# Attention steps that exponentiate heads in pairs and score four at a time, in place of groups of three

## The chip, the cores and the metric

One core of a Trainium2 chip runs the whole program. The metric is the device time of one execution in microseconds (us). Times "into the span" count from the first profiled instruction.

## The reference

An attention layer and a mixture-of-experts layer read the same normalised rows, and both are added to the input. Cut to what matters:

```python
xn = layernorm(x)                               # x: (4, 1024, 128)
q, k, v = heads(xn @ Wq.T), heads(xn @ Wk.T), heads(xn @ Wv.T)   # 16 heads of 8
q, k = rope(q), rope(k)
attn = softmax(einsum('bhnd,bhmd->bhnm', q, k) * 8 ** -0.5)
x = x + einsum('bhnm,bhmd->bhnd', attn, v) + moe(xn)   # 8 experts, 3 layers, top 2 by a gate
```

For each batch (4) and head (16), 1024 x 1024 scores are exponentiated: 67 million exponentials, all on ScalarE save some that VectorE takes in the last steps.

## The kernel before

**Steps and blocks.** Attention runs in 16 steps: a step is one batch and four of its heads. A step has 16 blocks (`BLOCKS`), numbered j: two halves of 512 queries, and in each half eight tiles of 128 keys. A block is one tile of keys against 512 queries for four heads. Its scores are four matmuls that contract 32 rows each (one head in each quarter of TensorE's rows) into 512 columns of a PSUM bank apiece; they are exponentiated by ScalarE from PSUM into `probs`; and its values are matmuls (eight in the trace, two for each head) that add the weighted values, and the sums by which to divide, into one bank (`o_ps`) that runs through the step.

**Steps 0 and 1** handle a block as two pairs of heads. `scores` (L1494 to L1519) writes the four heads of a block into two slots of two banks: pair 0 always into the same slot, pair 1 into one of two others in turn. It waits only for the exponentials of pair 0 of the block before. `attention_exps` (L716) runs two activations of 1024 columns for each block (L723). Every step has 32 of them. On ScalarE these two steps are a loop, whose waits compare with values worked out in registers.

**Steps 2 to 8** run through the 64 heads of a step (16 blocks of 4) in 22 groups of three, `group_scores` (L1610), two of the 22 having two heads. Two slots of three banks alternate: the scores of group g+1 wait for the exponentials of group g-1. `group_exps` (L730) runs one activation of 1536 columns for each group (L745), or of 1024 for a group of two. `group_values` (L1628) runs a block's values when the group that holds its fourth head is done, so that 16 of the 22 groups are followed by values and six are not. ScalarE's instructions for these steps are written out, with constants in their waits.

**Pieces.** Beside attention, TensorE runs work for later batches and for the experts, one piece after a block's or group's scores and before the values: transposes of rows (`rows`), projections of values and gates (`values`), rotary projections of later queries and keys (`plain`), norms for a safety bound (`norm`, `bound`), counts for the routing (`count`) and the transposes of the output of the step before (`turn`). The table `JOBS` of `plan_jobs` says which piece stands at which block of which step. In the steps with groups `JOB_PLACE` says after which group's scores the piece of block 0, 4, 6, 8, 12 or 14 runs: groups 1, 5, 9, 12, 16 and 20, which are the six that no values follow. `place` moves later pieces only to those blocks.

**Who waits.** TensorE's order in a step is written out (`step`, L1645, and the loop at L1747): scores of the next block or group, the piece, values of this one. VectorE copies the finished `o_ps` away at a step's end (`copy_o`, L1007), and the first values of the next step wait for that copy. SyncE loads the next step's queries and keys once the scores that read the old ones are done (L478, L482, L486).

**After step 8** the experts run (39 tiles, L1565 to L1586 on TensorE, GELUs at L759), then steps 9 to 15 in groups of three with help from VectorE (L1671, L1703, L780). The first expert layer of the first tile (`layer1(0, -2)`, L1565) stands before the values of step 8's last block; the transposes of that step's output follow them (`turn(SPLIT - 1)`, L1548), and then the second layer (L1573).

Of the kernel before, what the change touches and what calls it, by code (L numbers as in the profile page):

```python
# [24 lines left out]
P = 128  # L25
B, N, C = 4, 1024, 128
H, D = 16, 8
HG = 4
# [5 lines left out]
MT = N // P  # L34
# [13 lines left out]
HALF_GROUPS = -(-MT * HG // 3)  # L48
GROUPS = 2 * HALF_GROUPS
KEYS_READ = HALF_GROUPS + (MT * HG // 2 - 1) // 3 + 1  # L50
# [4 lines left out]
GROUPED = 2  # L55
# [26 lines left out]


def first_of(r, ending=False):

    return min(3 * r - (r == HALF_GROUPS - 1 and not ending), MT * HG)


def heads_of(g, ending=False):

    r = g % HALF_GROUPS
    return [divmod(n, HG) for n in range(first_of(r, ending), first_of(r + 1, ending))]


def place_of(mt, h, ending=False):

    n = HG * mt + h
    r = [r for r in range(HALF_GROUPS) if n >= first_of(r, ending)][-1]
    return r, n - first_of(r, ending)


def ends_steps(t, half):

    return t == SPLIT - 1 and half == 1


def block_ending_in(g):

    for mt, h in heads_of(g):
        if h == HG - 1:  # L110
            return g // HALF_GROUPS * MT + mt
    return None


def blocks_full(g):

    return g // HALF_GROUPS * MT + heads_of(g)[-1][0] + 1
# [53 lines left out]
JOB_PLACE = {1: 0, 5: 4, 9: 6, 12: 8, 16: 12, 20: 14}  # L171
# [7 lines left out]
def plan_jobs():  # L179
# [27 lines left out]
ROUTE_EXP = (2, 14)  # L207
# [19 lines left out]
def build(nc, x, Wq, Wk, Wv, w1, b1, w2, b2, w3, b3, gw, gb, rope_cos, rope_sin, consts, out):  # L227
    ctx = ExitStack()
    with ctx:
# [128 lines left out]
        def group_probs(phase, g):  # L358

            return probs[:].rearrange("p a h n -> p (a h) n")[:, 3 * ((2 * phase + g) % GROUP_RING):3 * ((2 * phase + g) % GROUP_RING) + 3, :]  # L360
# [25 lines left out]
        def _(sp):  # L386
# [86 lines left out]
            for t in range(SPLIT):  # L473
                for j in range(BLOCKS):
# [34 lines left out]
                    if t * BLOCKS + j in EXPERT_LOADS:  # L509
                        sp.wait_ge(S["scores_done"], group_units(t) + j * GROUPS // BLOCKS)  # L510
# [155 lines left out]
        def _(act):  # L666
# [60 lines left out]
            with act.Fori(0, GROUPED) as t:  # L727
                attention_exps(t)
            def group_exps(t, phase, first=False):
                for g in range(GROUPS):  # L730
                    if isinstance(t, int) and (t, g) == ROUTE_EXP:
                        act.wait_ge(S["max_made"], 1)
                        nc.scalar.activation(rt[:, 1], rt[:, 0], ACT.Exp).then_inc(S["exp_made"], 1)
                    act.wait_ge(S["scores_done"], group_units(t) + (g + 1))

                    if g >= GROUP_RING:
                        act.wait_ge(S["pv_done"], t * BLOCKS + (BLOCKS + blocks_full(g - GROUP_RING)))
                    elif first:
                        act.wait_ge(S["pv_done"], t * BLOCKS + BLOCKS)
                    elif isinstance(t, int) and t == GROUPED:  # L740
                        act.wait_ge(S["pv_done"], t * BLOCKS + (BLOCKS - PROB_RING + (3 * g + 2) // HG + 1))
                    else:
                        act.wait_ge(S["pv_done"], t * BLOCKS + blocks_full(g - GROUP_RING + GROUPS))
                    size = len(heads_of(g, ends_steps(t, g // HALF_GROUPS)))
                    nc.scalar.activation(group_probs(phase, g)[:, 0:size, :],  # L745
                                         group_slot(g)[:, 0:size * HALF].rearrange("p (h n) -> p h n", n=HALF),
                                         ACT.Exp, scale=SCALE).then_inc(S["exp_done"], 1)
# [644 lines left out]
        def _(pe):  # L1392
# [217 lines left out]
            def group_scores(t, g):  # L1610

                half = g // HALF_GROUPS
                pairs = heads_of(g, ends_steps(t, half))
                if g == 0:
                    pe.wait_ge(S["ka_loaded"], t * 16 + 16)
# [255 lines left out]
```

## Time and profile before

| what | value |
|---|---|
| median of three runs | 621.4 us (620.99 to 623.19) |
| the profiled execution's own time | 621.06 us |
| its span, first to last instruction | 619.5 us |
| granted TensorE clock over the span | 0.998 of full speed |
| TensorE matmuls busy | 588.0 us (95%) |
| ScalarE busy | 531.5 us (86%) |
| VectorE busy | 365.2 us (59%) |
| steps 2 to 8, from their first exponential to the end of their last | 84.56 to 292.77 us |

Busy shares are means over parts with different limits. Matmuls overlap and their ends are modelled, so that 95% of TensorE is not a full engine; in the attention steps ScalarE and TensorE hand work to each other every 1 to 2 us, and it takes the order of time in one step to see which of them the other waits for. An activation's row also covers the overlap with the next one, so that two that follow directly start closer together than one lasts.

### The profile page before, as it was taken

How to read it: one execution, taken by the hardware profiler on the slowest of the kernel's cores; microseconds unless marked ns; L12 is line 12 of the kernel's file. 1: busy time of each engine (PE TensorE's matmuls, PEld its weight loads, DVE VectorE, ACT ScalarE, POOL GpSimd, SP SyncE). 2: the span in 40 equal slices, each digit the busy share in tenths (PEclk: the TensorE clock that was granted, in tenths of full speed). 3: DMA queues.
4: the chain of work that ended last, by engine and by line, in shares of the span. 5: the costliest groups of instructions: out<-in, count | busy, mean ns of one | idle time of the engine just before them, and what ended most of it. 6: DMA issues, size and time to landing. Idle time of an engine off the chain costs nothing.

```text
span 619.5 us, 12074 instructions
## 1 busy us (share of the span) xinstructions
PE 588.0 (95%) x4106; PEld 252.2 (41%) x4106; DVE 365.2 (59%) x805; ACT 531.5 (86%) x541; POOL 211.6 (34%) x188
## 2 busy tenths in 40 slices
PE   7889999999999998999999999999999999999996
PEld 5323332222222222222899999993222222222221
DVE  5754224856462432121555555655778889898866
ACT  3699999999999999999455455559999999999995
POOL 2700000000554545442122222123867658686100
PEclk9999999999999999999999999999999999999999
DMA  8564601641464546492533333310212121221311
GB/s 234 159 217 168 241 34 52 222 171 52 154 221 162 176 139 205 146 302 54 123 74 78 74 75 77 75 44 18 78 66 90 43 78 60 64 76 64 115 47 38
DMA packets 83294, 70.68 MB, mean 114 GB/s; under 512 B 45344, under 2 KB 59072, under 8 KB 83248
## 3 DMA queue, kind: packets, MB, share of 16 engines
q1 hardware_dynamic: 76528, 56.47, 30.1%
q0 software_dynamic: 5856, 13.05, 6.7%
q10 hardware_dynamic: 864, 0.58, 0.4%
q8 instruction: 24, 0.39, 0.3%
q14 instruction: 22, 0.18, 0.1%
HBM read 32.92 MB, written 32.96 MB: 106 GB/s over the span
## 4 chain that ended last, share of the span: by engine, by line
PE 60%; DVE 17%; ACT 13%; issue 8%; DMA 1%; POOL 1%; ACTq 0%; SPq 0%; POOLq 0%; DVEq 0%
PE ps L1639 13%; PE ps L1573 10%; PE ps L1623 8%; DVE probs L1323 7%; ACT probs L745 7%; PE ps L1586 5%; PE ps L1565 5%; PE ps L1703 5%; ACT probs L780 4%; PE ps L1535 4%; PE ps L1671 3%; ACT probs L723 2%; DVE probs L1325 2%; DVE x_all L1266 2%; PE ps L1480 2%
## 5 line engine op out<-in xcount | busy, mean ns | idle before, releaser
L745 ACT ACTIVATE probs<-ps 128x1536 f32<-128x1536 f32 (+1 forms) x154 | 204.9, 1439 | 3.2 <-PE ps L1623 3.0
L780 ACT ACTIVATE probs<-ps 128x1536 f32<-128x1536 f32 x140 | 189.8, 1511 | 1.7 <-PE ps L1671 1.5
L621 POOL DMA_INDIRECT slots_x_d<-xn_all,slot_i x64 | 63.2, 988 | 191.5 <-PE ps L1639 181.1
L659 POOL DMA_INDIRECT work<-slots_y_d,slot_i x64 | 105.8, 1653 | 47.5 <-PE ps L1703 30.7
L1639 PE MATMUL ps<-probs,v_st 128*32 128x512 f32 x896 | 119.3, 605 | 0.6 <-ACT probs L745 0.6
L759 ACT ACTIVATE work<-ps,work 128x256 f32<-128x256 f32 (+1 forms) x156 | 64.9, 455 | 60.4 <-PE ps L1573 60.2
L1703 PE MATMUL ps<-probs,v_st 128*32 128x512 f32 x840 | 111.5, 604 | 0.0
L1623 PE MATMUL ps<-q_st,k_st 32*128 32x512 f32 x448 | 76.3, 494 | 5.9 <-ACT probs L745 5.7
L1671 PE MATMUL ps<-q_st,k_st 32*128 32x512 f32 x420 | 71.1, 494 | 7.7 <-ACT probs L780 7.2
L1623 PEld LDWEIGHTS ps<-q_st,k_st 32*128 32x128 f32 x448 | 28.9, 181 | 117.5 <-ACT probs L745 102.4
L1671 PEld LDWEIGHTS ps<-q_st,k_st 32*128 32x128 f32 x420 | 26.5, 181 | 106.8 <-ACT probs L780 98.8
L1573 PE MATMUL ps<-work 128*128 128x256 f32 (+1 forms) x312 | 67.9, 361 | 0.0
L723 ACT ACTIVATE probs<-ps 128x1024 f32<-128x1024 f32 x64 | 60.6, 1035 | 4.9 <-PE ps L1515 4.0
L640 POOL DMA_DIRECT2D slots_y_d<-work x39 | 26.7, 685 | 110.0 <-DVE work L1183 105.5
L1573 PEld LDWEIGHTS ps<-work 128*128 128x128 f32 x312 | 53.0, 191 | 5.0
L1323 DVE SCALAR_TENSOR_TENSOR probs<-probs,work 128x2048 f32<-128x2048 f32 (+1 forms) x21 | 46.5, 2215 | 0.7
L1586 PE MATMUL ps<-work 128*128 128x128 f32 x284 | 38.2, 275 | 0.0
L1586 PEld LDWEIGHTS ps<-work 128*128 128x128 f32 x284 | 37.2, 191 | 1.9 <-issue 0.2
L1535 PE MATMUL ps<-probs,v_st 128*32 128x512 f32 x256 | 34.1, 604 | 3.7 <-ACT probs L723 2.3
L1565 PE MATMUL ps<-work 128*128 128x256 f32 (+1 forms) x156 | 37.2, 361 | 0.0
L1307 DVE TENSOR_SCALAR work<-ps 128x512 f32<-128x512 f32 x27 | 18.6, 690 | 20.4 <-PE ps L1686 20.4
L1565 PEld LDWEIGHTS ps<-work 128*128 128x128 f32 x156 | 27.9, 190 | 4.1 <-ACT probs L745 0.8
(206 smaller groups left out, 541.3 us busy)
## 6 DMA issues: line engine op xcount, KB each, us to landing
k_d<-parts SPq DMA_DIRECT2D x8, 1024.0 KB, 5.2
q_d<-parts SPq DMA_DIRECT2D x8, 1024.0 KB, 6.1
q_st<-q_d SPq DMA_DIRECT2D x30, 256.0 KB, 3.6
k_st<-k_d SPq DMA_DIRECT2D x30, 256.0 KB, 2.7
slots_x_d<-parts SPq DMA_DIRECT2D x5, 1024.0 KB, 7.9
work<-slots_x_d SPq DMA_DIRECT2D x128, 32.0 KB, 1.9
slots_y_d<-work POOLq DMA_DIRECT2D x32, 128.0 KB, 2.2
work<-work SPq DMA_DIRECT2D x24, 128.0 KB, 2.0
```

The source lines that it names most:

```text
L659: nc.gpsimd.indirect_dma_start(out=gath[:, i % 2, GATHER * c + k, :], out_offset=None, in_=slots_y_d, in_offset=bass.IndirectOffsetOnAxis( ...
L723: nc.scalar.activation(probs[:, j % PROB_RING, 2 * pair:2 * pair + 2, :], score_slot(j, pair).rearrange("p (h n) -> p h n", h=2), ACT.Exp, ...
L745: nc.scalar.activation(group_probs(phase, g)[:, 0:size, :], group_slot(g)[:, 0:size * HALF].rearrange("p (h n) -> p h n", n=HALF), ACT.Exp ...
L780: nc.scalar.activation(late_probs(g), group_slot(g).rearrange("p (h n) -> p h n", n=HALF), ACT.Exp, scale=SCALE).then_inc(S["exp_done"], 1)
L1323: ins = nc.vector.scalar_tensor_tensor(power, rest if k == 3 else power, EXP_COEFFS[k - 3], rest, ALU.add, ALU.mult)
L1565: nc.tensor.matmul(h1_ps[m][:, 0:units * ST], w1_sb[:, n % 2, m * P:(m + 1) * P], xsT[:, n % 2, 0:units * ST], start=True, stop=True).then ...
L1573: ins = nc.tensor.matmul(h2_ps[m][:, 0:units * ST], w2_sb[:, n % 2, k, m * P:(m + 1) * P], h1[:, n % 2, k, 0:units * ST], start=(k == 0), ...
L1586: ins = nc.tensor.matmul(y_ps[par][:, m, 0:C], h2[:, par, k, m * P:(m + 1) * P], w3_sb[:, par, k, :], start=(k == 0), stop=(k == 1))
L1623: ins = nc.tensor.matmul(group_slot(g)[:, n * HALF:(n + 1) * HALF], k_st[32 * h:32 * h + ROWS, mt * P:(mt + 1) * P], q_st[32 * h:32 * h + ...
L1639: ins = nc.tensor.matmul(o_ps[32 * h:32 * h + 32, :], v_window(mt, h, half), group_probs(phase, half * HALF_GROUPS + g)[:, n, :], start=(j ...
L1671: ins = nc.tensor.matmul(group_slot(g)[:, n * HALF:(n + 1) * HALF], k_st[32 * h:32 * h + ROWS, mt * P:(mt + 1) * P], q_st[32 * h:32 * h + ...
L1703: ins = nc.tensor.matmul(dst[32 * h:32 * h + 32, :], v_window(mt, h, half), late_probs(g)[:, k, :], start=begins, stop=ends)
```

## The change

Steps 2 to 8 take the same functions as steps 0 and 1: `scores`, `attention_exps` and `values`. Groups of three are gone from them, with the functions that place heads in groups (`first_of`, `heads_of`, `place_of`, `group_probs`, `group_exps`, `group_scores`, `group_values`, `step`). A step now has 32 activations of 1024 columns in place of 20 of 1536 and two of 1024, and 16 rounds of scores with four heads in place of 22. On ScalarE step 2 is written out and steps 3 to 8 are a loop. `JOB_PLACE` is gone: a piece runs in the block that `JOBS` names, and `place` may use any free block. Waits by the count of scores follow the new count of 32 for each step. The gates' exponential (`ROUTE_EXP`, L733) moves from group 14 to block 10 of step 2, and four banks of the expert layers are exchanged (`h1_ps`, `h2_ps`).

```diff
 def group_units(t):
     if not isinstance(t, int) or t > SPLIT:
-        return t * LATE_GROUPS + (SPLIT * (GROUPS - LATE_GROUPS) + GROUPED * (UNITS - GROUPS))
-    if isinstance(t, int) and t < GROUPED:
-        return t * UNITS
-    return t * GROUPS + GROUPED * (UNITS - GROUPS)
+        return t * LATE_GROUPS + SPLIT * (UNITS - LATE_GROUPS)
+    return t * UNITS
...
-JOB_PLACE = {1: 0, 5: 4, 9: 6, 12: 8, 16: 12, 20: 14}
...
-        while n in turns or n in fixed or (n >= BLOCKS * GROUPED and n % BLOCKS not in JOB_PLACE.values()):
+        while n in turns or n in fixed:
             n += 1
...
-ROUTE_EXP = (2, 14)
+ROUTE_EXP = (2, 10)
...
-        h1_ps, h2_ps = [bank(2), bank(5)], [bank(3), bank(4)]
+        h1_ps, h2_ps = [bank(2), bank(3)], [bank(4), bank(5)]
...
-                        sp.wait_ge(S["scores_done"], group_units(t) + (HALF_GROUPS if t >= GROUPED else UNITS // 2))
+                        sp.wait_ge(S["scores_done"], t * UNITS + UNITS // 2)
                         load_half(q_st, q_d, t + 1, 0, S["q0_loaded"])
...
-                        sp.wait_ge(S["scores_done"], group_units(t) + (KEYS_READ if t >= GROUPED else 3 * UNITS // 4))
+                        sp.wait_ge(S["scores_done"], t * UNITS + 3 * UNITS // 4)
                         load_half(k_st, k_d, t + 1, 0, S["ka_loaded"])
...
                     act.wait_ge(S["scores_done"], t * UNITS + (u + 1))
+                    if isinstance(t, int) and (t, j) == ROUTE_EXP and pair == 0:
+                        act.wait_ge(S["max_made"], 1)
+                        nc.scalar.activation(rt[:, 1], rt[:, 0], ACT.Exp).then_inc(S["exp_made"], 1)
...
-            with act.Fori(0, GROUPED) as t:
+            with act.Fori(0, ROUTE_EXP[0]) as t:
                 attention_exps(t)
...
-            group_exps(GROUPED, 0)
-            for t in range(GROUPED + 1, SPLIT):
-                group_exps(t, t % 2)
+            attention_exps(ROUTE_EXP[0])
+            with act.Fori(ROUTE_EXP[0] + 1, SPLIT) as t:
+                attention_exps(t)
...
-            for t in range(GROUPED):
+            for t in range(SPLIT):
                 for j in range(BLOCKS):
                     if j < BLOCKS - 1:
                         scores(t, j + 1)
-                    elif t < GROUPED - 1:
+                    elif t < SPLIT - 1:
                         scores(t + 1, 0)
                     else:
-                        group_scores(t + 1, 0)
+                        pe.wait_ge(S["exp_done"], group_units(SPLIT) - 1)
+                        layer1(0, -2)
...
-            for t in range(GROUPED, SPLIT):
-                step(t, t % 2, last=(t == SPLIT - 1), joined=(t == GROUPED))
-            pe.wait_ge(S["exp_done"], group_units(SPLIT) - 1)
-            layer1(0, -2)
-            group_values(SPLIT - 1, BLOCKS - 1, (SPLIT - 1) % 2)
             turn(SPLIT - 1)
```

TensorE's order in step 4, around the piece `plain` of block 8, before. L1623 is scores, L1639 values, L1548 `turn`, L1480 `plain`.

```order
L1548 MATMUL ps<-cst,o_sb 128x128 x4
L1623 MATMUL ps<-q_st,k_st 128x512 x3
L1639 MATMUL ps<-probs,v_st 32x512 x4
L1623 MATMUL ps<-q_st,k_st 128x512 x3
L1639 MATMUL ps<-probs,v_st 32x512 x4
L1623 MATMUL ps<-q_st,k_st 128x512 x3
L1480 MATMUL ps<-work,wT 128x512
L1623 MATMUL ps<-q_st,k_st 128x512 x3
L1639 MATMUL ps<-probs,v_st 32x512 x4
```

The same place of the change, where L1451 is scores, L1471 values, L1484 `turn` and L1416 `plain`.

```order
L1484 MATMUL ps<-cst,o_sb 128x128 x4
L1471 MATMUL ps<-probs,v_st 32x512 x4
L1451 MATMUL ps<-q_st,k_st 128x512 x4
L1471 MATMUL ps<-probs,v_st 32x512 x4
L1451 MATMUL ps<-q_st,k_st 128x512 x4
L1416 MATMUL ps<-work,wT 128x512
L1471 MATMUL ps<-probs,v_st 32x512 x4
```

Before, no values stand between the scores ahead of a piece and those behind it; now every piece stands between the four scores and the values of a block. The pieces keep their blocks: the table `JOBS` comes out the same in both kernels.

TensorE's order at the end of step 8, before: L1565 is the first expert layer, L1573 the second.

```order
L1623 MATMUL ps<-q_st,k_st 128x512 x3
L1639 MATMUL ps<-probs,v_st 32x512 x4
L1623 MATMUL ps<-q_st,k_st 128x512 x2
L1639 MATMUL ps<-probs,v_st 32x512 x4
L1565 MATMUL ps<-work 128x256 x2
L1639 MATMUL ps<-probs,v_st 32x512 x4
L1548 MATMUL ps<-cst,o_sb 128x128 x4
L1573 MATMUL ps<-work 128x256 x4
```

And in the change, with L1501 and L1509 for the two layers.

```order
L1451 MATMUL ps<-q_st,k_st 128x512 x4
L1471 MATMUL ps<-probs,v_st 32x512 x4
L1501 MATMUL ps<-work 128x256 x2
L1471 MATMUL ps<-probs,v_st 32x512 x4
L1484 MATMUL ps<-cst,o_sb 128x128 x4
L1509 MATMUL ps<-work 128x256 x4
```

The order there is the same; what differs is which exponential the values ahead of the expert layer (block 14's) wait for. Before it is the last but one of the step, a group of three that holds the fourth head of block 14 and two of block 15. Now it is pair 1 of block 14, the third from the end.

## Rows read from the trace of the kernel before

**Rows 1.** Windows, steps 1, 4, 2 to 8: length, busy by engine, clock, DMA share, GB/s.
```profile
53.24:84.56 31.32, 30.33 (x236) 10.78 (x236) 9.68 (x31) 30.49 (x32) 0.00 (x0) 1.00 0.56 201
...
144.21:174.05 29.84, 29.21 (x205) 7.98 (x202) 16.40 (x41) 29.39 (x22) 9.55 (x10) 1.00 0.34 116
...
84.56:292.77 208.21, 201.70 (x1441) 56.08 (x1441) 86.85 (x221) 205.04 (x156) 63.23 (x64) 1.00 0.46 154
```

**Rows 2.** Timeline of TensorE in step 4: start, length, line, instructions merged.
```profile
161.95 0.50 PE L1623 MATMUL ps<-q_st,k_st 32*128 32x512 f32 x3
162.38 1.13 PE L1480 MATMUL ps<-work,wT 128*128 128x512 f32 x2
163.44 0.50 PE L1623 MATMUL ps<-q_st,k_st 32*128 32x512 f32 x3
163.87 1.06 PE L1639 MATMUL ps<-probs,v_st 128*32 128x512 f32 x8
164.86 0.50 PE L1623 MATMUL ps<-q_st,k_st 32*128 32x512 f32 x3
```

**Rows 3.** Timeline of ScalarE: exponentials in step 4, step 2, then step 0.
```profile
146.89 10.86 ACT L745 ACTIVATE probs<-ps 128x1536 f32<-128x1536 f32 x8
...
156.21 1.54 ACT L745 ACTIVATE probs<-ps 128x1536 f32<-128x1536 f32 x1
...
104.11 0.44 ACT L733 ACTIVATE rt<-rt 128x256 f32<-128x256 f32 x1
104.41 1.47 ACT L745 ACTIVATE probs<-ps 128x1536 f32<-128x1536 f32 x1
...
26.06 12.94 ACT L723 ACTIVATE probs<-ps 128x1024 f32<-128x1024 f32 x14 [0.97 <-PE ps L1515]
...
37.93 1.07 ACT L723 ACTIVATE probs<-ps 128x1024 f32<-128x1024 f32 x1
39.31 1.02 ACT L723 ACTIVATE probs<-ps 128x1024 f32<-128x1024 f32 x1 [0.31 <-PE ps L1515]
```

**Rows 4.** Timeline of TensorE in step 0, around the piece `norm` of block 7.
```profile
36.40 0.51 PE L1515 MATMUL ps<-q_st,k_st 32*128 32x512 f32 x4
36.83 0.62 PE L1448 MATMUL ps<-squares,head_r 128*32 128x512 f32 x2
...
37.72 1.04 PE L1535 MATMUL ps<-probs,v_st 128*32 128x512 f32 x8
38.69 0.51 PE L1515 MATMUL ps<-q_st,k_st 32*128 32x512 f32 x4
...
42.30 0.51 PE L1515 MATMUL ps<-q_st,k_st 32*128 32x512 f32 x4
```

**Rows 5.** Timeline of TensorE in step 1: scores of blocks 3, 5 to 7, 9; a piece.
```profile
58.69 0.51 PE L1515 MATMUL ps<-q_st,k_st 32*128 32x512 f32 x4
...
62.41 0.50 PE L1515 MATMUL ps<-q_st,k_st 32*128 32x512 f32 x4
...
64.42 0.51 PE L1515 MATMUL ps<-q_st,k_st 32*128 32x512 f32 x4
...
66.52 0.51 PE L1515 MATMUL ps<-q_st,k_st 32*128 32x512 f32 x4
66.95 0.73 PE L1437 MATMUL ps<-wvg,work 128*128 128x136 f32 x4
67.61 1.06 PE L1535 MATMUL ps<-probs,v_st 128*32 128x512 f32 x8
...
70.31 0.50 PE L1515 MATMUL ps<-q_st,k_st 32*128 32x512 f32 x4
```

**Rows 6.** Timeline of TensorE from the end of step 8 into the experts.
```profile
291.91 1.07 PE L1639 MATMUL ps<-probs,v_st 128*32 128x512 f32 x8 [0.58 <-ACT probs L745]
292.90 1.13 PE L1565 MATMUL ps<-work 128*128 128x256 f32 x4
293.96 1.06 PE L1639 MATMUL ps<-probs,v_st 128*32 128x512 f32 x8
295.94 0.63 PE L1548 MATMUL ps<-cst,o_sb 128*128 128x128 f32 x4 [0.91 <-DVE o_sb L1007]
```

More of the change, by code:

```diff
@@ L47 @@
 BLOCKS = 2 * MT
-HALF_GROUPS = -(-MT * HG // 3)
-GROUPS = 2 * HALF_GROUPS
-KEYS_READ = HALF_GROUPS + (MT * HG // 2 - 1) // 3 + 1
 GROUP_RING = 4
@@ L54 @@
 SPLIT = 9
-GROUPED = 2
 GATHER = 6
@@ L81, in slot_tile @@
     return i * CYCLE + (n + 2), 2, i * (CYCLE - 2) * 2 + (n + 2 - singles) * 2, i * (CYCLE - 2) + (n + 2 - singles)
[L84 to L117, printed above, removed]
 LATE_BLOCKS = [(0, mt) for mt in range(1, MT)] + [(1, mt) for mt in range(MT)]
@@ L356, in build @@
         he_p = help_probs.rearrange("p h n -> p (h n)")
-        def group_probs(phase, g):
-            return probs[:].rearrange("p a h n -> p (a h) n")[:, 3 * ((2 * phase + g) % GROUP_RING):3 * ((2 * phase + g) % GROUP_RING) + 3, :]
         y_ps = [bank(k, 2).rearrange("p (k c) -> p k c", k=2) for k in (6, 0)]
-        h1_ps, h2_ps = [bank(2), bank(5)], [bank(3), bank(4)]
+        h1_ps, h2_ps = [bank(2), bank(3)], [bank(4), bank(5)]
         names = """x_loaded0 x_loaded0b x_loaded1 x_loaded2 x_loaded3 weights_loaded small_loaded gate_loaded rope_loaded0 rope_loaded1 bias_loaded
@@ L509, in _ @@
                     if t * BLOCKS + j in EXPERT_LOADS:
-                        sp.wait_ge(S["scores_done"], group_units(t) + j * GROUPS // BLOCKS)
+                        sp.wait_ge(S["scores_done"], t * UNITS + 2 * j)
                         load_expert(EXPERT_LOADS.index(t * BLOCKS + j))
@@ L725, in attention_exps @@
                                          ACT.Exp, scale=SCALE).then_inc(S["exp_done"], 1)
-            with act.Fori(0, GROUPED) as t:
+            with act.Fori(0, ROUTE_EXP[0]) as t:
                 attention_exps(t)
[L729 to L747, printed above, removed]
-            group_exps(GROUPED, 0)
-            for t in range(GROUPED + 1, SPLIT):
-                group_exps(t, t % 2)
+            attention_exps(ROUTE_EXP[0])
+            with act.Fori(ROUTE_EXP[0] + 1, SPLIT) as t:
+                attention_exps(t)
             def gelus(i, tile):
@@ L1608, in extra_piece @@
                     turn_bound()
[L1610 to L1615, printed above, removed]
-                    pe.wait_ge(S["q0_loaded"], t * 16 + 16)
-                if half == 0 and (MT // 2, 0) in pairs:
-                    pe.wait_ge(S["kb_loaded"], t * 16 + 16)
-                if g == HALF_GROUPS:
-                    pe.wait_ge(S["q1_loaded"], t * 16 + 16)
-                pe.wait_ge(S["exp_done"], group_units(t) + (g - 1))
-                for n, (mt, h) in enumerate(pairs):
-                    ins = nc.tensor.matmul(group_slot(g)[:, n * HALF:(n + 1) * HALF],
-                                           k_st[32 * h:32 * h + ROWS, mt * P:(mt + 1) * P],
-                                           q_st[32 * h:32 * h + ROWS, half * HALF:(half + 1) * HALF], start=True, stop=True)
-                ins.then_inc(S["scores_done"], 1)
@@ L1628, in group_values @@
-            def group_values(t, j, phase):
-                half, mt = divmod(j, MT)
-                last = [g for g in range(GROUPS) if block_ending_in(g) == j][0]
-                pe.wait_ge(S["exp_done"], group_units(t) + (last + 1))
-                if j in (0, 4):
-                    pe.wait_ge(S["v_loaded"], t * 2 + (j // 4 + 1))
-                if j == 0:
-                    pe.wait_ge(S["o_copied"], t)
-                for h in range(HG):
-                    g, n = place_of(mt, h, ends_steps(t, half))
-                    ins = nc.tensor.matmul(o_ps[32 * h:32 * h + 32, :], v_window(mt, h, half),
-                                           group_probs(phase, half * HALF_GROUPS + g)[:, n, :], start=(j == 0), stop=(j == BLOCKS - 1))
-                ins.then_inc(S["pv_done"], 1)
@@ L1643, in step @@
-            def step(t, phase, last=False, joined=False):
-                for g in range(GROUPS):
-                    if g < GROUPS - 1:
-                        group_scores(t, g + 1)
-                    elif not last:
-                        group_scores(t + 1, 0)
-                    if g in JOB_PLACE:
-                        extra_piece(t, JOB_PLACE[g])
-                    if g > 0:
-                        j = block_ending_in(g - 1)
-                        if j is not None:
-                            group_values(t, j, phase)
-                    elif not joined:
-                        group_values(t - 1, BLOCKS - 1, 1 - phase)
@@ L1750, in _ @@
                         scores(t, j + 1)
-                    elif t < GROUPED - 1:
+                    elif t < SPLIT - 1:
                         scores(t + 1, 0)
                     else:
-                        group_scores(t + 1, 0)
+                        pe.wait_ge(S["exp_done"], group_units(SPLIT) - 1)
+                        layer1(0, -2)
                     if (t, j) == (0, 0):
```

## The prediction

> **What bounds the kernel now.** I read the busy times of the page first, then windows of single steps, then the timeline of TensorE and of ScalarE inside them, since a mean over the span hides the hand-over.
>
> Steps 2 to 8 take 208.21 us from their first exponential to the end of their last, and ScalarE is busy for 205.04 of them [rows 1]. So ScalarE looks like the bound. But its rows also cover waits too short to show. Where TensorE is in time, eight groups start 146.89 to 156.21, seven distances of 1.331 us [rows 3]. Twenty such groups and two of two heads (about 0.91 each, as a pair takes) make 28.4 us. Step 4 takes 29.84 [rows 1]. The missing 1.4 is TensorE: scores 163.44, values 163.87, scores 164.86, with nothing between [rows 2], is a round of 1.42 us, slower than ScalarE's 1.33. It falls behind after a piece and stays behind until a group without values lets it catch up. The piece itself is cheap there: from the scores at 161.95 to those at 163.44 is 1.49 us with a whole `plain` of 1.06 in it, because no values follow [rows 2].
>
> Steps 0 and 1 already run the new way, so that the trace shows the price of it. Undisturbed, 14 exponentials of 1024 columns start from 26.06 to 37.93, thirteen distances of 0.913 us [rows 3], 1.826 for a block. TensorE's block is scores 0.43 and values 0.97 (36.40 to 36.83, 37.72 to 38.69 [rows 4]), 1.40 in all. It has about 0.43 to spare for a piece.
>
> **The exponentials.** 7 steps of 32 at 0.913 are 204.5 us. The same columns in groups are 7 x 28.4 = 199.1. The fixed part of 66 more instructions is therefore 5.4 us, on the path, since ScalarE is the engine that both kernels keep supplied.
>
> The Trainium skill has a rule that speaks against this edit too (ScalarE: Activation LUTs, "What ACT_TABLE_LOAD costs"): an activation with immediate scale and bias takes 186 ns and 0.833 ns a column, and successive ones overlap by about 93 ns. By it, as an estimate, 1024 columns cost 0.946 us and 1536 cost 1.373, the difference over seven steps is 6.4, and the time below would be 1.0 higher. The trace's 0.913 and 1.331 are both lower, and are used.
>
> **Scores.** Six rounds fewer a step. Three heads or four take TensorE the same 0.43 us (161.95 to 162.38 [rows 2], 36.40 to 36.83 [rows 4]), so a step gives TensorE 6 x 0.43 = 2.6 us back. That is a gain only where TensorE is late, and shows in the pieces' price, next.
>
> **Pieces.** They keep their blocks; "free places" moves none, so that part costs and gives nothing. Each now stands between scores and values of a block that has both. What one costs alone is read from the distances between scores, against 1.826 a block:
> - `norm`, 0.89 long: 36.40 to 42.30, three blocks, 5.90 for 5.48 [rows 4]: 0.42. ScalarE's idle 0.31 at 39.31 [rows 3] is its share.
> - `values`, 0.66 long: 66.52 to 70.31, two blocks, 3.79 for 3.65 [rows 5]: 0.14. Right behind another piece: 64.42 to 66.52, 2.10 for 1.83: 0.27.
> - four transposes: 58.69 to 62.41, 3.72 for 3.65 [rows 5]: 0.07.
>
> So a piece costs its length less about half a microsecond. `plain` (1.06 long [rows 2]) was never run in such a block. Its price lies between `norm`'s 0.42 (a shorter piece) and its whole 1.06. A gain is excluded, since it adds work to the engine that is late. I take 0.60, `norm`'s price and the 0.17 that it is longer, `norm` being the nearest row. Steps 2 to 8 have 12 `plain` (7.2), one `count`, taken like `plain` (0.6), 3 `norm` (1.26), 7 `turn` (0.49), one `bound`, taken like `turn` (0.07), and 2 `values`, one right behind another piece (0.27 and 0.14): 10.0 us. The gates' exponential moves four tenths of a step and still delays by 0.30 (104.11 to 104.41 [rows 3]). The last exponential ends 0.16 after its share (1.07 less 0.91 [rows 3]).
>
> Steps 2 to 8 then take 204.5 + 10.0 + 0.3 + 0.2 = 215.0 in place of 208.2: **6.8 us more**.
>
> **The hand-over to the experts.** Before, the values ahead of the first expert layer wait until 291.91 for the last exponential but one (0.58 idle), the layer runs at 292.90, the last values at 293.96, the turn at 295.94 [rows 6]: 3.17 after the last exponential's end at 292.77. Now those values wait for the third exponential from the end. With 0.91 each, they start about 1.8 before the end, the layer 0.8 before it, the last values 0.3 after it, and the turn 1.98 later, as now: 2.3 after the end. This gives **0.9 us** back, or none if the next things (the first tile's rows, VectorE's staging) are late. I take it: that work was ready before 292.90.
>
> Costed at nothing: loads of queries and keys, the same count of blocks ahead of their use; registers for waits in ScalarE's loop, which are in the rows of steps 0 and 1; the exchanged banks; everything after the turn, which shifts as a whole.
>
> **Sum:** 621.06 (the profiled execution's own time) + 6.8 - 0.9 = **627.0 us**. The median of the runs shown is 621.4, within 0.1% of that execution. A measurement of this kernel tells about 0.5%, 3.1 us, from no change.
>
> **Rivals.**
> 1. *TensorE's relief decides (faster).* If 2.6 us a step cover all the pieces, which come to 3.8 at most in a step, ScalarE alone sets the pace: 204.5 + 0.5 = 205.0, 3.2 less than now, and 0.9 at the hand-over: 617.0 us. It decides where a block absorbs a whole `plain`, 1.06 in place of 0.43. For it: four-deep rows are used in full, and steps 2 to 8 lose 9 us to TensorE now. Against: step 1 has the same relief and takes 31.32 us with ten short pieces [rows 1], 2.1 over its 32 exponentials. The Trainium skill argues for this side (TensorEngine Tiling (Array Packing), "Theoretical Speedup"): a dimension of at most 32 gives up to four times the work in a pass, which three heads do not use. The trace agrees on the rounds, 0.43 either way, and not on who is late. Chance 0.07.
> 2. *Only the fixed part counts.* The pieces cost in pairs what all of TensorE's lateness costs in groups, 208.2 - 199.1 = 9.1, since the lag is made good in the free blocks: 204.5 + 9.1 - 208.2 - 0.9 = 4.5 more, 625.6 us. It needs `plain` near `norm`'s price. Chance 0.18.
> 3. *A new wait.* The pieces share one PSUM bank that VectorE must have read before the next may run. Two blocks, 3.7 us, now part `plain` at block 12 and `turn` at block 14 of step 2, and other pairs stand as close; a microsecond late in four such places is paid in full: 631 us. It decides when VectorE's queue is more than two blocks late. Against: VectorE is busy for 16.40 of 29.84 us in step 4 [rows 1]. Chance 0.10.
> 4. That the change does not do what it says holds for one half (free places); it has no price and no chance of its own.
>
> **How the numbers follow.** The forecast has 0.65. The range takes in the second rival and the low end of `plain` (12 x 0.18 = 2.2 less, 624.8), and upward the hand-over without gain (627.9) and about half of the way to the high end of `plain` (12 x 0.46 = 5.5 more): 624.2 to 630.6. Outside lie the first rival and most of the third. Faster by over 0.5% (under 618.3): the first rival, 0.07. Within 0.5%: the low tail of the second, 0.07. Slower (over 624.5): the rest, 0.86.
>
> **What would show it.** Right: an activation of 1024 columns every 0.91 us in all nine steps; steps 3 to 6 near 31 us; after every `plain` an idle of ScalarE of 0.3 to 0.5 us released by TensorE's scores; free blocks of 1.83; the turn about 2.3 us after the last exponential. Wrong: steps of 29.2 us with no idle (first rival); distances over 2.6 us between scores around a `plain`, or TensorE's piece released by VectorE (third rival); a longer experts' stage.

## The result, and the profile of the changed kernel

The changed kernel takes **630.72 us** (median of 4 runs, 629.87 to 632.84) against 621.19 (4 runs, 620.72 to 623.19) for the kernel before: a ratio of **1.0151 [1.0124, 1.0179]**, slower. The forecast was 627.0, within 624.2 to 630.6: the sign was right, and the time lies 0.1 us above the range. The profiled execution took 631.56 us, 10.5 more than that of before; its span is 629.8.

The windows of the changed kernel, for steps 2, 3, 4 and 7 and for steps 2 to 8, with the columns of [rows 1]:

```profile
84.78:116.53 31.75, 29.26 (x214) 8.37 (x214) 13.65 (x31) 30.25 (x34) 0.00 (x0) 1.00 0.24 83
...
116.53:150.66 34.13, 29.01 (x210) 7.44 (x210) 20.43 (x62) 29.82 (x33) 0.00 (x0) 0.95 0.38 135
...
150.66:181.83 31.17, 27.56 (x202) 6.91 (x202) 16.42 (x41) 29.76 (x33) 10.15 (x11) 1.00 0.33 113
...
243.98:273.82 29.84, 25.42 (x204) 6.30 (x204) 5.26 (x13) 29.61 (x33) 13.84 (x15) 1.00 0.57 191
...
84.78:303.81 219.03, 191.82 (x1444) 49.98 (x1444) 86.48 (x221) 208.66 (x226) 63.22 (x64) 0.99 0.44 146
```

Steps 2 to 8 are 10.8 us longer than before [rows 1]; 215.0 had been expected, 219.0 came. TensorE's busy time fell by 9.9 us, and the steps grew all the same. Step 4 is 31.17, "near 31" as forecast. Step 3 is not: 34.13, at a granted clock of 0.95, with VectorE at 20.43.

ScalarE's timeline in steps 4 and 5 (start, length, exponentials that follow directly, the idle time before):

```profile
170.27 7.44 ACT L679 ACTIVATE probs<-ps 128x1024 f32<-128x1024 f32 x8 [0.41 <-PE ps L1451]
178.20 7.44 ACT L679 ACTIVATE probs<-ps 128x1024 f32<-128x1024 f32 x8 [0.49 <-PE ps L1451]
186.13 14.90 ACT L679 ACTIVATE probs<-ps 128x1024 f32<-128x1024 f32 x16 [0.49 <-PE ps L1451]
```

Eight exponentials take (7.44 - 1.07) / 7 = 0.91 us each; then comes an idle time of 0.4 to 0.5 that the scores end. From 170.27 to 178.20 are 7.93 us, 0.63 more than eight times 0.913: the price of one `plain`, that of block 12. TensorE's timeline around the `plain` of block 8 shows where such a price arises:

```profile
167.16 0.51 PE L1451 MATMUL ps<-q_st,k_st 32*128 32x512 f32 x4
167.59 1.12 PE L1416 MATMUL ps<-work,wT 128*128 128x512 f32 x2
168.65 1.06 PE L1471 MATMUL ps<-probs,v_st 128*32 128x512 f32 x8
169.65 0.51 PE L1451 MATMUL ps<-q_st,k_st 32*128 32x512 f32 x4
```

The scores stand 2.49 us apart (167.16 to 169.65), with scores, piece and values back to back, where ScalarE needs 1.83 for a block; those around block 12 stand 2.49 apart as well. So far this is the forecast. What it lacks lies at the start of step 3. TensorE's timeline there comes first, then VectorE's, then ScalarE's:

```profile
110.21 1.12 PE L1416 MATMUL ps<-work,wT 128*128 128x512 f32 x2
...
116.63 1.06 PE L1471 MATMUL ps<-probs,v_st 128*32 128x512 f32 x8 [0.22 <-ACT probs L679]
117.63 0.50 PE L1451 MATMUL ps<-q_st,k_st 32*128 32x512 f32 x4
118.06 1.13 PE L1416 MATMUL ps<-work,wT 128*128 128x512 f32 x2
121.20 1.84 PE L1471 MATMUL ps<-probs,v_st 128*32 128x512 f32 x8 [2.01 <-DVE v_st L841]
122.97 0.80 PE L1451 MATMUL ps<-q_st,k_st 32*128 32x512 f32 x4
```

```profile
111.78 0.69 DVE L918 TENSOR_TENSOR work<-ps,work 128x512 f32<-128x512 f32 x1 [3.76 <-PE ps L1416]
...
118.55 0.41 DVE L991 TENSOR_REDUCE rs<-rt 128x32 f32<-128x256 f32 x1
...
119.91 0.42 DVE L995 TENSOR_REDUCE gates<-rt 128x32 f32<-128x256 f32 x1
120.36 0.69 DVE L943 COPY o_sb<-ps 128x512 f32<-128x512 f32 x1
120.97 0.22 DVE L841 COPY v_st<-v_all 128x128 f32<-128x128 f32 x1
```

```profile
123.88 15.01 ACT L679 ACTIVATE probs<-ps 128x1024 f32<-128x1024 f32 x16 [3.58 <-PE ps L1451]
```

The first values of step 3 wait for VectorE's copy of the finished sums (`copy_o`, L943). The row names L841, the copy that stands directly behind it in VectorE's order; by the program these values wait for `copy_o` and for the first half of the step's v, which was copied at 112.99. The last values of step 2 are done at 117.7, but VectorE works without a pause from 111.78, on the products and joins of the `plain` of block 12 (TensorE 110.21) and on parts of the routing (L985 to L995), and reaches the copy at 120.36, 2.7 us late. TensorE stands still for 2.01 us. Then its clock drops: the granted clock is 1.00 from 119.20 to 121.20, the 3.8 us behind the stall run at a mean of 0.55, and values take 1.84 and scores 0.80 in place of 1.06 and 0.50. The window:

```profile
121.10:124.90 3.80, 3.70 (x20) 0.68 (x20) 3.66 (x8) 1.02 (x2) 0.00 (x0) 0.55 0.43 160
```

ScalarE idles for 3.58 us ahead of the exponential at 123.88, 3.2 more than the 0.41 behind a like `plain` (170.27). The kernel before has the same chain on VectorE, of the same length (109.96 to 118.56, 8.6 us both times):

```profile
108.39 1.12 PE L1480 MATMUL ps<-work,wT 128*128 128x512 f32 x2
...
116.62 1.06 PE L1639 MATMUL ps<-probs,v_st 128*32 128x512 f32 x8
...
119.10 0.50 PE L1623 MATMUL ps<-q_st,k_st 32*128 32x512 f32 x3
119.53 1.07 PE L1639 MATMUL ps<-probs,v_st 128*32 128x512 f32 x8
```

```profile
109.96 0.69 DVE L982 TENSOR_TENSOR work<-ps,work 128x512 f32<-128x512 f32 x1 [1.39 <-PE ps L1480]
...
118.56 0.69 DVE L1007 COPY o_sb<-ps 128x512 f32<-128x512 f32 x1
```

What differs most is the distance from that `plain` to the step's last values: 8.23 us before, 6.42 now. In groups it stands in group 16 of 22; in pairs it stands in block 12 of 16, nearer to the end. The cover behind those values has shrunk too: before, TensorE had a `plain` and one more round of scores to run (to 119.53), now it has the `plain` alone (to 119.19). The 1.8 us of distance and 0.3 of cover, less the 0.1 to spare before, are the 2.0 of the stall.

The hand-over to the experts came as forecast. TensorE's timeline at the end of step 8:

```profile
302.03 1.07 PE L1471 MATMUL ps<-probs,v_st 128*32 128x512 f32 x8 [0.33 <-ACT probs L679]
303.02 1.13 PE L1501 MATMUL ps<-work 128*128 128x256 f32 x4
304.08 1.06 PE L1471 MATMUL ps<-probs,v_st 128*32 128x512 f32 x8
306.06 0.63 PE L1484 MATMUL ps<-cst,o_sb 128*128 128x128 f32 x4 [0.91 <-DVE o_sb L943]
```

The turn starts 2.25 us after the last exponential's end at 303.81, in place of 3.17 [rows 6]. It is 306.06 - 295.94 = 10.12 later than before, and from there on everything is shifted as a whole: the first exponential of the late steps comes 10.12 later too.

### The profile page after: what moved, and what is told of

Same layout as the page of the kernel before. It is cut to its first block, busy times and chain, and to the rows that moved or that the text cites. A ratio compares the mean times of both kernels' runs of the same rounds, so it can differ in the third digit from the quotient of the medians.

```text
span 629.8 us, 12307 instructions
## 1 busy us (share of the span) xinstructions
PE 577.1 (92%) x4106; PEld 245.3 (39%) x4106; DVE 364.6 (58%) x805; ACT 535.1 (85%) x611; POOL 211.7 (34%) x188
## 4 chain that ended last, share of the span: by engine, by line
PE 47%; ACT 19%; DVE 18%; issue 13%; ACTq 1%; DMA 1%; POOL 1%; SPq 0%; DVEq 0%; POOLq 0%
ACT probs L679 15%; PE ps L1509 10%; PE ps L1471 9%; DVE probs L1259 7%; PE ps L1522 5%; PE ps L1501 5%; PE ps L1591 5%; PE ps L1451 4%; ACT probs L716 4%; PE ps L1559 3%; PE ps L1416 2%; DVE probs L1261 2%; DVE x_all L1202 2%; DVE work L1255 1%; PE ps L1373 1%
## 5 line engine op out<-in xcount | busy, mean ns | idle before, releaser
L679 ACT ACTIVATE probs<-ps 128x1024 f32<-128x1024 f32 x288 | 268.9, 1047 | 15.0 <-PE ps L1451 14.0
L1471 PE MATMUL ps<-probs,v_st 128*32 128x512 f32 x1152 | 154.8, 609 | 27.6 <-ACT probs L679 22.9
L1559 PE MATMUL ps<-q_st,k_st 32*128 32x512 f32 x420 | 71.1, 494 | 7.3 <-ACT probs L716 7.1
L1451 PE MATMUL ps<-q_st,k_st 32*128 32x512 f32 x576 | 73.1, 496 | 4.9 <-ACT probs L679 3.8
L1451 PEld LDWEIGHTS ps<-q_st,k_st 32*128 32x128 f32 x576 | 27.9, 182 | 127.4 <-ACT probs L679 101.8
L1509 PE MATMUL ps<-work 128*128 128x256 f32 (+1 forms) x312 | 68.0, 361 | 0.0
L1509 PEld LDWEIGHTS ps<-work 128*128 128x128 f32 x312 | 53.0, 191 | 5.0
L1471 PEld LDWEIGHTS ps<-probs,v_st 128*32 128x32 f32 x1152 | 23.4, 108 | 73.6 <-ACT probs L679 67.7
L1501 PE MATMUL ps<-work 128*128 128x256 f32 (+1 forms) x156 | 37.2, 361 | 0.0
L1501 PEld LDWEIGHTS ps<-work 128*128 128x128 f32 x156 | 27.9, 190 | 4.1 <-ACT probs L679 0.8
L918 DVE TENSOR_TENSOR work<-ps,work 128x512 f32<-128x512 f32 x12 | 8.3, 690 | 36.6 <-PE ps L1416 36.6
```

Of the source, the lines that this page charges most:

```text
L679: nc.scalar.activation(probs[:, j % PROB_RING, 2 * pair:2 * pair + 2, :], score_slot(j, pair).rearrange("p (h n) -> p h n", h=2), ACT.Exp, ...
L1451: ins = nc.tensor.matmul(score_slot(j, h // 2)[:, (h % 2) * HALF:(h % 2 + 1) * HALF], k_st[32 * h:32 * h + ROWS, mt * P:(mt + 1) * P], q_s ...
L1471: ins = nc.tensor.matmul(o_ps[32 * h:32 * h + 32, :], v_window(mt, h, half), probs[:, j % PROB_RING, h, :], start=(j == 0), stop=(j == BLO ...
L1501: nc.tensor.matmul(h1_ps[m][:, 0:units * ST], w1_sb[:, n % 2, m * P:(m + 1) * P], xsT[:, n % 2, 0:units * ST], start=True, stop=True).then ...
L1509: ins = nc.tensor.matmul(h2_ps[m][:, 0:units * ST], w2_sb[:, n % 2, k, m * P:(m + 1) * P], h1[:, n % 2, k, 0:units * ST], start=(k == 0), ...
L1559: ins = nc.tensor.matmul(group_slot(g)[:, n * HALF:(n + 1) * HALF], k_st[32 * h:32 * h + ROWS, mt * P:(mt + 1) * P], q_st[32 * h:32 * h + ...
```

## The experiments

The theory is a sum of three: 5.4 us of fixed part, 0.6 for each `plain` in a block that is full already, and the late copy with its clock. Rivals were a cost of entering ScalarE's loop (step 3 is its first turn) and dearer waits on its registers throughout. Further runs ask whether the pieces' price can be taken away, and what it is in groups.

**Routing work out of the copy's way.**

```diff
-ROUTE = {divmod(block, BLOCKS): n for n, block in enumerate((39, 43, 44, 45, 46, 47, 49, 51, 53, 57, 58, 59, 60, 61, 62, 63, 64, 65, 66, 67, 68))}
+ROUTE = {divmod(block, BLOCKS): n for n, block in enumerate((39, 43, 44, 48, 49, 50, 51, 52, 53, 57, 58, 59, 60, 61, 62, 63, 64, 65, 66, 67, 68))}
```

> Changed kernel, but VectorE's routing parts 3 to 8 are spread over blocks 48 to 53 (from block 0 of step 3), so that parts 3, 4 and 5 no longer stand ahead of the copy of step 2's output. Theory: at the end of step 2 VectorE's queue is late, TensorE waits 2.0 us for the copy and then runs 3.4 us at the lower clock; the 3.7 us extra at block 2 of step 3 falls to about 0.6 (the plain piece alone), the granted clock is 1.00 there, and the time falls by about 3 us against the changed kernel, to about 628. Rival (entry into ScalarE's loop at step 3 is what costs): no change, the stall stays at 3 us or more.

Measured: 628.13 us (628.07 to 629.49), 1.0093 [1.0058, 1.0129] of before. Steps 2 to 8, then VectorE and TensorE at the boundary:

```profile
84.92:300.70 215.78, 190.26 (x1444) 49.81 (x1444) 86.56 (x221) 208.56 (x226) 63.07 (x64) 1.00 0.45 149
```

```profile
117.15 0.69 DVE L939 TENSOR_TENSOR squares<-work 128x512 f32<-128x512 f32 x1
117.90 0.69 DVE L943 COPY o_sb<-ps 128x512 f32<-128x512 f32 x1
```

```profile
118.20 1.13 PE L1416 MATMUL ps<-work,wT 128*128 128x512 f32 x2
119.25 1.07 PE L1471 MATMUL ps<-probs,v_st 128*32 128x512 f32 x8
```

The copy runs as soon as the last values of step 2 are done (117.83), and the first values follow the `plain` at once. The granted clock from 119.20 to 124.00 is 1.00. Step 3 falls from 34.13 to 30.89 with ScalarE's loop as it was, so the loop's entry costs nothing that shows. What is left, 215.8, is the sum of the prediction (215.0) within 0.8 us.

**ScalarE's loop written out.**

```diff
-            with act.Fori(ROUTE_EXP[0] + 1, SPLIT) as t:
+            for t in range(ROUTE_EXP[0] + 1, SPLIT):
                 attention_exps(t)
```

> Changed kernel with ScalarE's steps 3 to 8 written out in place of the loop, nothing else. Theory: the loop costs only where ScalarE is idle, 0.07 us each time for a register's value that is worked out behind the first wait (0.62 us from scores to exponential against 0.55): some 24 delayed exponentials, 1.7 us less than the changed kernel, about 629; the 3 us stall at the start of step 3 stays. Rival (the loop's entry is the stall): the stall goes and the time falls by 3 us or more. Second rival (registers cost nothing): no change.

Measured: 629.24 us (628.13 to 631.33), 1.0108 [1.0066, 1.0149]; steps 2 to 8 take 217.53, 1.5 less than in the changed kernel, and the stall is still there: the block that it falls in is 3.8 us longer than a free one, 3.7 in the changed kernel. The intervals of the two times overlap, so that the 1.5 rests on one profile of each. TensorE's scores and the exponential that waits for them:

```profile
169.11 0.51 PE L1451 MATMUL ps<-q_st,k_st 32*128 32x512 f32 x4
```

```profile
169.66 2.85 ACT L679 ACTIVATE probs<-ps 128x1024 f32<-128x1024 f32 x3 [0.36 <-PE ps L1451]
```

0.55 us lie between the two, 0.62 in the changed kernel (169.65 and 170.27 above). So this exponential, which has to wait, starts 0.07 later when its wait compares with registers; those that need not wait come every 0.913 us either way. The prediction had this inside the price of pieces, whose rows come from a loop too.

**Pieces behind the values instead of ahead of them.**

```diff
-                    else:
+                    elif t < 2:
                         extra_piece(t, j)
                         values(t, j)
+                    else:
+                        values(t, j)
+                        extra_piece(t, j)
```

> Changed kernel with the piece of steps 2 to 8 behind the values of its block, in place of ahead of them. Theory (what a block has to spare is TensorE's idle time ahead of the values, while it waits for the exponential of pair 1): the piece loses that cover and costs its whole length, about 0.45 us more for each of 26 pieces, some 10 to 12 us more than the changed kernel, about 642. Rival (the slack is per block, wherever the piece stands): the same time.

Measured: 644.51 us (one run; the changed kernel 630.72), and 232.25 for steps 2 to 8. The window of these steps comes first, then TensorE around a `plain`:

```profile
84.65:316.90 232.25, 193.35 (x1444) 50.35 (x1444) 86.70 (x221) 208.67 (x226) 62.38 (x64) 0.99 0.42 138
```

```profile
174.84 1.07 PE L1471 MATMUL ps<-probs,v_st 128*32 128x512 f32 x8 [0.41 <-ACT probs L679]
175.84 1.13 PE L1416 MATMUL ps<-work,wT 128*128 128x512 f32 x2
176.89 0.51 PE L1451 MATMUL ps<-q_st,k_st 32*128 32x512 f32 x4
```

TensorE now idles 0.41 ahead of the values, time that the piece had filled, and each `plain` costs 1.0 to 1.3 us; the stall at the start of step 3 grows with it, from 3.7 us to 5.7. So the place between scores and values is the better of the two: it hides 0.4 to 0.6 of a piece.

**Pieces in halves, over two blocks** (with the routing moved as above).

```diff
+SPLIT_JOBS = [at for at, job in JOBS.items() if at[0] >= 2 and (job[0] in ("norm", "count", "bound") or job[0] == "plain" and at[1] != 12)]
...
+                if (t, j) in SPLIT_JOBS:
+                    cut = 1
+                elif (t, j - 1) in SPLIT_JOBS:
+                    job, cut = JOBS[(t, j - 1)], 2
+                if cut and job[0] == "plain":
+                    project(job[1], ((0, HALF // 2),) if cut == 1 else ((HALF // 2, HALF),))
...
```

> The kernel of e1_routes, and the pieces plain of blocks 0, 4 and 8, the norms, count and bound of steps 2 to 8 are cut in two halves of about 0.5 us, run in two successive blocks. Theory (a piece costs its length less about half a microsecond, each block having that much to spare): nine plain fall from 0.6 to about 0.15 (4.1 us), three norms, the count and the bound give 1.7 more: 5.5 to 6 us less than e1_routes, about 622, with steps 4 and 6 near 30.2. Rival (a piece costs by its mere presence, or the whole of its length): no change against e1_routes.

Measured: 627.07 us (626.84 to 628.71), 1.0078 [1.0054, 1.0101]; steps 2 to 8 take 214.96, only 0.8 less than with the routing alone. This is a miss, and it says something on sizes. These are TensorE's scores around one `norm`, which is now run as a half in each of two blocks:

```profile
140.26 0.50 PE L1462 MATMUL ps<-q_st,k_st 32*128 32x512 f32 x4
...
142.54 0.51 PE L1462 MATMUL ps<-q_st,k_st 32*128 32x512 f32 x4
...
144.81 0.51 PE L1462 MATMUL ps<-q_st,k_st 32*128 32x512 f32 x4
```

The two blocks take 2.28 and 2.27 us for 1.83, so that each half costs about what the whole `norm` did (0.47). Two of its four matmuls last as long as all four: from the start of the `norm` to that of the values are 0.87 us for a half (140.70 to 141.57) and 0.88 for the whole (141.44 to 142.32 with the routing moved alone). The four write different column groups, and in the trace they start in pairs 0.02 us apart (141.44 and 141.46). Half a `plain` is 0.63 long, not half of 1.06, and the two halves together still cost 0.33 to 0.47 where a whole one costs 0.52 to 0.67.

**Quarters**, with the loop written out and the routing moved: every `plain` of steps 2 to 8 in four parts over four blocks (two at block 12), `turn` and `bound` in two parts.

```diff
...
+    if job[0] == "plain":
+        return {0: [0, 1, 2, 3], 4: [1, 2, 3, 4], 8: [7, 8, 9, 10], 12: [11, 12]}[j]
+    return {"turn": [5, 6] if j == 6 else [j], "bound": [0, 1]}.get(job[0], [j])
...
```

> The kernel of e1_routes with ScalarE's steps written out (as e2_written_out) and pieces cut finer: plain in four quarters of 128 columns in four successive blocks (two halves at blocks 11 and 12 for those of block 12), turns of block 6 and the bound in two halves; norms and count whole, since e3_split showed that two matmuls of a norm last as long as four. From 1.06 us for 512 columns and 0.63 for 256 a quarter is estimated at 0.42 us, about what a block has to spare. Theory (each block has some 0.35 to 0.5 us to spare, and ScalarE's 32 exponentials are the floor): steps 4 and 6 fall from 31.2 to about 29.7, steps 2 to 8 from 215.8 to about 208.8, the time from 628 to about 621, level with the kernel before and not under it by more than 0.5%. Rival (a piece costs by its presence): 626 or more, as e3_split.

Measured: 636.15 us (633.29 to 637.0), 1.0227 [1.0201, 1.0253], a miss as a whole. The windows of steps 4 and 5 come first, then a quarter of step 5 on TensorE:

```profile
154.38:189.07 34.69, 30.32 (x216) 9.35 (x216) 16.42 (x41) 29.88 (x33) 10.41 (x11) 0.95 0.29 100
189.07:219.19 30.12, 28.46 (x220) 8.67 (x220) 13.09 (x27) 29.67 (x34) 13.54 (x15) 1.00 0.57 196
```

```profile
192.67 0.49 PE L1434 MATMUL ps<-work,wT 128*128 128x128 f32 x2
193.09 1.06 PE L1494 MATMUL ps<-probs,v_st 128*32 128x512 f32 x8
```

Most quarters of step 5 show the price that was hoped for: a quarter is 0.42 long, from its start to that of the values, and costs up to 0.07. The one directly behind the `turn` costs 0.42, since it waits 0.40 for VectorE. A piece that lasts four blocks holds the one bank that all pieces share for as long, and its results come later. In step 4 VectorE had idled until the last quarter of block 0's `plain` was done; then it worked through its order and read the `turn` (L972) only at 171.74, and TensorE waited for that read. At the end of step 2 TensorE waited for a load of keys:

```profile
162.26 0.69 DVE L935 TENSOR_TENSOR work<-ps,work 128x512 f32<-128x512 f32 x1 [5.66 <-PE ps L1434]
```

```profile
172.28 0.49 PE L1434 MATMUL ps<-work,wT 128*128 128x128 f32 x2 [3.26 <-DVE attn_all L972]
```

```profile
117.71 0.51 PE L1474 MATMUL ps<-q_st,k_st 32*128 32x512 f32 x4 [1.70 <-DMA k_st<-k_d]
```

In step 3 the `count` waited 3.85 us for VectorE's read of the `turn` as well (L972, done at 138.38; the `count` starts at 138.43). Steps 3 and 4 lost 6.6 and 4.8 us to these waits and to the clock behind them, 0.52 from 138.40 to 143.00 and 0.65 from 172.30 to 176.50. This is the wait that the third rival described, a shared bank that VectorE has not read yet. It came once a piece lasted longer, and at other pairs of pieces than the one that the rival named.

**Quarters only where nothing waits for them**: the pieces of step 3 are whole again, and of those of steps 2 and 4 only the `plain` of blocks 4 and 8 are cut. The edit is shown against the kernel with quarters.

```diff
-    if t < 2:
+    if t < 2 or t == 3 or (t in (2, 4) and (job[0] != "plain" or j in (0, 12))):
         return [j]
+    if t == 4:
+        return [8, 9, 10, 11]
```

> The kernel of e5_quarters, with the pieces of step 3, of block 12 of step 2 and all of step 4 but the plain of block 8 whole again and in the places of the changed kernel (plain of block 8 of step 4 in quarters at blocks 8 to 11). Theory: the stalls of e5_quarters (1.8 us at the end of step 2, 6.7 in step 3, 4.8 in step 4) are VectorE's and SyncE's queues, held in order behind a piece that ends three blocks later; with the pieces whole there they go, steps 5 and 6 stay near 30.1, steps 2 to 8 take about 211.5 and the time is about 624, still over the kernel before. Rival (cutting itself brings the stalls): one of the three stays.

Measured: 626.35 us (625.13 to 626.88), 1.0081 [1.0065, 1.0096]; steps 2 to 8 take 212.19:

```profile
86.14:298.33 212.19, 194.22 (x1488) 56.31 (x1488) 86.25 (x221) 207.84 (x226) 63.10 (x64) 1.00 0.46 151
```

The stalls of steps 3 and 4 are gone; of that at the end of step 2, a wait for keys, 0.9 us stays. By its steps 2 to 8 it is the best version in pairs here that does all the work, and still 4.0 us above the kernel before in them.

**What a `plain` costs in either form.** In both kernels the 12 `plain` project 128 of their 512 columns, and the rest of these projections is left out.

```diff
-                nc.tensor.matmul(aux_ps, weights(g, 0), xnT[:, b, lo:lo + HALF], start=True, stop=True).then_inc(S["aux_done"], 1)
+                nc.tensor.matmul(aux_ps[:, 0:P], weights(g, 0), xnT[:, b, lo:lo + P], start=True, stop=True).then_inc(S["aux_done"], 1)
```

In groups:

> Kernel before (groups of three), with each of the 12 plain pieces projecting 128 of its 512 columns, which VectorE then reads four times: three quarters of the later rotary projections are left out, and a plain lasts about 0.42 us in place of 1.06. Theory: in groups the pieces stand where no values follow and TensorE's lateness is spread over the rounds of 1.42 us behind them; the shorter plain gives back about 0.3 us each, 3 to 4 us, 617 to 618. Rival (in groups a plain is hidden): no change.

In pairs, with the routing moved:

> The kernel of e1_routes with the same cut of the 12 plain pieces (three quarters of the later rotary projections left out). Theory: a plain of 0.42 us fits into what a block has to spare; its 0.55 to 0.67 goes nearly whole, 6.5 to 7 us, about 621.5, and steps 4 and 6 take some 29.5. Rival (a piece costs by its presence): a fall of under 3 us.

Measured: 619.0 and 621.53 us (one run each). Steps 2 to 8, groups and then pairs:

```profile
86.46:290.55 204.09, 195.09 (x1441) 56.21 (x1441) 86.78 (x221) 202.76 (x156) 63.65 (x64) 1.00 0.48 157
```

```profile
84.75:294.41 209.66, 183.38 (x1444) 49.98 (x1444) 86.38 (x221) 207.65 (x226) 62.43 (x64) 1.00 0.46 153
```

The three quarters of a `plain` that were taken away were worth (208.2 - 204.1) / 12 = 0.34 us each in groups and (215.8 - 209.7) / 12 = 0.51 in pairs. With them gone, pairs are 5.6 us longer than groups: about the fixed part, 5.4, since what is left of lateness is nearly the same, 209.7 - 204.5 = 5.2 in pairs and 204.1 - 199.1 = 5.0 in groups. The time in groups shows 2.4 of the 4.1 us that its steps gave, because that one execution came to step 2 at 86.46, 1.9 us after the kernel before.

**Halves in groups**: in the kernel before, steps 4 to 6 put `turn` at group 5 and the `plain` of group 12 in halves at groups 9 and 12.

```diff
...
+                    if t in (4, 5, 6) and g in (5, 9, 12):
+                        if g == 5:
+                            extra_piece(t, 6)
+                        else:
+                            project(JOBS[t, 8][1], (9, 12).index(g), 2)
...
```

> Kernel before (groups of three); in steps 4, 5 and 6 the turn moves from group 9 to group 5, which no values follow and which was free, and the plain of group 12 is cut into two halves of 256 columns (0.63 us each) at groups 9 and 12. Theory: a half and the scores of a group, 1.06 us, fit under an exponential of 1.33, so that TensorE is no longer late behind group 12, only behind the plain or norm of group 16: about 0.5 us less in each of the three steps, 1 to 2 us in all, steps 4 and 6 near 29.3, some 619.5 us; less than 0.5%, so the verdict by time may be open and the steps decide. Rival (the lag behind group 16 alone sets the step): no change in the steps.

Measured: 621.03 us (620.37 to 622.68, 11 runs), 0.9995 [0.9981, 1.0008]: no change that can be told. Steps 4 to 6 take 29.67, 29.55 and 29.61 for 29.84, 29.77 and 29.83, 0.2 a step where 0.5 was expected. The four rounds behind group 12 are in time now, 0.33 us less in all; those behind group 16 are as late as they were, and 0.16 is lost again at group 9, where a half now stands in place of the `turn` (from that group's exponential to the next are 1.23 us, 1.07 before).

No version in pairs that does all the work came down to the kernel before. ScalarE alone takes 32 x 0.913 = 29.2 us for a step in pairs and 28.4 in groups, so that with all of its idle time gone a step in pairs stands 0.6 under the 29.84 that groups take with theirs.

## Why the prediction was right and wrong

The profiled executions differ by 10.5 us, the prediction's terms came to 5.9.

- **The fixed part, 5.4: right.** The exponentials come every 0.91 us in steps 2 to 8, and the two kernels with short `plain` differ by 5.6, with as much lateness left in either. The Trainium skill's figures (ScalarE: Activation LUTs, "What ACT_TABLE_LOAD costs") gave 6.4, as an estimate; the trace's 0.91 us an exponential keeps the fixed part below that.
- **`plain`, 0.60: right.** In the kernel with the routing moved eleven of them cost 0.52 to 0.67, mean 0.60; the twelfth, behind which the gates' exponential stands, costs 0.82 with it. In the changed kernel that of block 0 of step 3 costs 3.7, with the stall in it. `norm`, taken from its own row, cost 0.34 to 0.47 for 0.42, `count` 0.54 for 0.60, and the `values` 0.27 and 0.07 for 0.27 and 0.14.
- **`turn` and `bound`, 0.07: too low.** Six of the seven `turn`, those at block 6, cost 0.19 to 0.20, 0.12 more each; the one at block 14 of step 2 cost the 0.07 of the forecast. Why the place in the step matters stays open. `bound` cost 0.44. Both were sized from the four transposes of step 1 [rows 5]. Together this is 1.1 us; other terms came out a little lower, and the kernel with the routing moved exceeds 215.0 by 0.8.
- **The hand-over, 0.9: right**, 0.92.
- **The step that failed** is the answer to the third rival: "VectorE is busy for 16.40 of 29.84 us in step 4". On the strength of it the prediction put no wait for VectorE into its sum and gave the rival a chance of 0.10. A mean over a step says nothing on where in VectorE's order an instruction stands, and step 4 was not the step to ask: in step 3 of the kernel before (115.63 to 145.56) VectorE is busy for 19.72 of 29.93 us. At the boundary of steps 2 and 3 VectorE was booked for 8.6 us in a row, and the copy that TensorE needs stood last. The kernel before was already 0.9 late there (last values done at 117.7, copy at 118.56), covered by a `plain` and a round of scores. The change cut the distance from 8.23 to 6.42 and the cover to the `plain`, which was short by 2.0 us. With the clock behind it the price was 3.2 us: 219.03 - 215.78. The rival named the `turn` behind the `plain` of this very block; that `turn` ran in time (114.33), and the copy at the step's end did not. One of the signs that the prediction gave for it came true at block 0 of step 3, scores more than 2.6 us apart: 117.63 and 122.97. The time of 630.7 lies next to the 631 at which the rival was priced; that is luck, since the price stood for four places of a microsecond each and the runs show one place of 3.2. The prediction could have worked this pair out, since both its ends were in the trace: a `plain` late in a step with 8.6 us of VectorE's work behind it, and the copy.
- **The first rival** (TensorE's relief decides) falls. The relief is there, 9.9 us of busy time over steps 2 to 8, but a block that holds a `plain` and values is longer on TensorE than its exponentials on ScalarE by 0.66 us, and the four-deep rows do not change that. The Trainium skill (TensorEngine Tiling (Array Packing), "Theoretical Speedup") gives up to four times for a dimension of at most 32. The trace agrees in that TensorE's busy time fell; no run here turned it into time. **The second** (pieces cost no more than all lateness in groups) falls by 2.2 us: 215.78 - 208.21 = 7.6 with the stall removed, of which 5.4 are fixed. In groups a piece has a group without values to stand in, and a `plain`'s three quarters are worth 0.17 less there; twelve times that is 2.0.
- **The fourth**, that free places do nothing, holds: no piece moved to another block.

The difference of the profiled executions adds up: 5.4 fixed, 2.2 pieces, 3.2 stall and clock, less 0.9 at the hand-over, with 0.2 at the start of step 2 and 0.2 in the late steps: 10.3, the difference of the spans.

Not tried: pairs with fine pieces where VectorE's and SyncE's order in steps 2 to 4 is planned anew. It could take the last 0.9 us of waiting from the best version in pairs, which would still leave it above the kernel before.

## What to carry to other kernels

In this kernel relief of TensorE gave nothing and a fixed price on ScalarE, the engine that both forms keep supplied, was paid in full. The price per instruction of the new form was in the trace, in two steps that already ran it, and held (0.913 us). What a re-timed step can break is found by following each wait across its in-order queue: for every producer whose consumer moves nearer, add up the work queued between the two on the engine that links them, and set it against the new distance. A mean busy share does not show this.

## What the runs showed of the hardware

- A pause of 2.01 us in TensorE's work was followed by 3.8 us at a mean granted clock of 0.55, most of them at the lower of its two levels, 1.2 GHz in place of 2.4. Stall and clock together cost 3.2 us, so that the lower clock cost some 1.2 us more, over half of what the stall itself lasted. The waits of 3.26 and 3.85 us in the kernel with quarters were followed by the lower level as well (0.65 and 0.52).
- An exponential that waits for scores started 0.07 us later when its waits compare with registers than when they compare with constants (0.62 and 0.55 us after the scores' start, step 4, behind the `plain` of block 8).
- A part of a piece does not shrink when its columns are cut: 512, 256 and 128 columns last 1.06, 0.63 and 0.42 us in the traces, from the start to that of the next instruction. The steps of 0.43 and 0.21 leave about 0.2 us that each piece pays whatever its columns (an estimate from the three).
- The four matmuls of a `norm`, which write different column groups, took 0.88 us, and two of them alone 0.87.
